# Expert loop of a two-layer kernel: rows turned by a transposing DMA, second product two tiles behind the first

## The reference

```
gate_scores = softmax(x @ Wg + bg);  topk_scores, topk_idx = top_k(gate_scores, 2)
for e in range(8):
    h = gelu(x @ W1[e] + b1[e])          # 128 -> 512
    y = h @ W2[e] + b2[e]                # 512 -> 128
    output = output + y * combine_w[..., e]
```

## Time and profile before

| | us |
|---|---|
| median of 3 runs | 1599.52 (1598.59 to 1602.85) |
| the profiled execution's own time | 1598.53 |
| its span, first to last instruction | 1596.6 |
| PE busy in the span | 1392.2 (87%) |
| DVE busy | 1355.3 (85%) |
| ACT busy | 1280.3 (80%) |
| POOL busy | 1079.0 (68%) |

### The profile page before, as it was taken

One profiled execution on the slowest core, in us unless ns is written; L12 is line 12 of the kernel. 1 busy time (PEld: TensorE's weight loads), 2 busy tenths in 40 slices (PEclk: granted clock), 3 DMA queues, 4 the chain that ended last, 5 costly groups with the idle time before them and its releaser, 6 DMA issues. The chain is left out here.

```text
span 1596.6 us, 53031 instructions
## 1 busy us (share of the span) xinstructions
PE 1392.2 (87%) x17084; PEld 1186.1 (74%) x17084; DVE 1355.3 (85%) x3979; ACT 1280.3 (80%) x3930; POOL 1079.0 (68%) x1524
## 2 busy tenths in 40 slices
PE   4779889974799999999999999999999719999970
PEld 3667777763688888888888888888888618888860
DVE  4479999995799999999999999999999628888877
ACT  1358888875799999999999999999999616666645
POOL 0367877763666577887788778877887555666650
PEclk7989999986899999999999999999999959999995
DMA  5445553400100000000000000000000013332209
GB/s 145 140 158 180 192 202 148 160 2 5 27 13 12 13 20 20 23 22 19 18 22 22 18 18 22 22 18 18 22 15 9 22 43 91 87 84 77 80 28 316
DMA packets 99738, 101.83 MB, mean 64 GB/s; under 512 B 15305, under 2 KB 81132, under 8 KB 99457
## 3 DMA queue, kind: packets, MB, share of 16 engines
q1 hardware_dynamic: 82496, 78.77, 15.4%
q0 software_dynamic: 8640, 16.93, 3.2%
q10 hardware_dynamic: 8448, 4.20, 0.9%
HBM read 39.40 MB, written 57.16 MB: 60 GB/s over the span
## 5 line engine op out<-in xcount | busy, mean ns | idle before, releaser
L1227 ACT ACTIVATE c_p<-bank,c_nmax 128x128 f32<-128x128 f32 x1024 | 368.9, 401 | 2.2 <-DVE c_nmax L1081 1.3
L1016 POOL TENSOR_TENSOR c_p<-c_p,c_rden 128x512 f32<-128x512 f32 x256 | 266.8, 1042 | 110.4 <-DVE c_rden L1091 106.0
L1227 ACT ACTIVATION_READ_ACCUMULATOR c_p<-bank,c_nmax 128x1 f32 x1024 | 244.2, 241 | 0.0
L1403 POOL DMA_INDIRECT moe_outputs<-e_y,e_to x142 | 152.9, 1077 | 93.3 <-DVE e_y L1434 58.6
L112 PE MATMUL bank<-c_kvT,qk_fused 128*128 128x128 f16 x1024 | 185.8, 220 | 10.8 <-ACT c_kvT L1206 10.4
L1081 DVE TENSOR_REDUCE c_nmax<-bank 128x4 f32<-128x512 f32 x256 | 173.4, 677 | 17.5 <-PE bank L114 14.3
L114 PE MATMUL bank<-c_kvT,qk_fused 128*128 128x128 f16 x1024 | 185.7, 220 | 0.0
L113 PE MATMUL bank<-c_kvT,qk_fused 128*128 128x128 f16 x1024 | 185.7, 220 | 0.0
L1473 ACT ACTIVATE e_h<-bank,moe_b 128x256 f32<-128x256 f32 x284 | 117.9, 466 | 65.7 <-PE bank L114 64.4
L1297 PE MATMUL bank<-const,c_p 128*128 128x128 f32 x1024 | 155.9, 275 | 3.6 <-DVE c_pT0rest L1102 1.7
L1059 POOL DMA_INDIRECT moe_slots<-r_rows,r_pos x128 | 131.6, 1028 | 34.9 <-issue 34.9
(11 more groups left out here) (324 smaller groups left out, 5921.0 us busy)
## 6 DMA issues: line engine op xcount, KB each, us to landing
moe_slots<-slot_fill SPq DMA_DIRECT2D x66, 520.0 KB, 5.6
e_rows<-moe_slots SPq DMA_DIRECT2D x71, 130.0 KB, 2.2
f_z<-moe_outputs SPq DMA_DIRECT2D x32, 256.0 KB, 4.9
x<-in_x SPq DMA_DIRECT2D x16, 256.0 KB, 3.2
a_ctx<-in_ctx SPq DMA_DIRECT2D x32, 128.0 KB, 3.4
moe_stage<-in_L_ffn_W SPq DMA_DIRECT2D x16, 256.0 KB, 3.1
c_rows<-in_ctx SPq DMA_DIRECT2D x128, 32.0 KB, 2.0
c_rows<-x SPq DMA_DIRECT2D x128, 32.0 KB, 1.8
```

The lines of the kernel that those rows point to most:

```text
L1016: pool.tensor_tensor(pr[r % 4][:], pr[r % 4][:], rep(rden[r % 4][:], 2, P), ALU.mult).then_inc(m["pn"], 1)
L1227: last = act.activation(pr[r % 4][:, h, :], SB[r % 2][:, P * h:P * h + P], ACT.Exp, bias=nmax[r % 4][:, h:h + 1], accum_out=den[r % 4][:, ...
L1403: pool.indirect_dma_start(s.z, bass.IndirectOffsetOnAxis(ap=to[t % YBUF][:, h:h + 1], axis=0), ys[t % YBUF][:, h, :], None, bounds_check=2 ...
```

## The change

SP issues two DMAs per tile where it issued one: a transposing one of the first 256 values of each slot, straight into `e_xT` (now 6 buffers, free again when the first product of tile t-6 is through), and a plain one of the last 4 half floats into `e_dest` (12 buffers). PE's `turn` and DVE's `spread` go away with their semaphores, and the two banks that they used go to the first product, which now turns over 6 banks instead of 4. `second` and `finish` run two tiles behind instead of one; the parts of h get a third set. The weights are addressed through a view with an axis for the expert, instead of `e * FF + P * b`.

```diff
-XBUF, YBUF = 12, 6
+XBUF, DBUF, YBUF = 6, 12, 6
...
-    hs = [[sb(f"e_hs{n}{part}", [P, KB, TSLOT], F16) for part in ("high", "rest")] for n in range(2)]
+    hs = [[sb(f"e_hs{n}{part}", [P, KB, TSLOT], F16) for part in ("high", "rest")] for n in range(3)]
...
-    HB, YB = s.pb[0:4], s.pb[4:6]
-    XTB = [s.pb[6][:].bitcast(F16), s.pb[7][:].bitcast(F16)]
+    HB, YB = s.pb[0:6], s.pb[6:8]
+    by_expert = wts[:].rearrange("p a (e f) -> p a e f", e=EXPERTS)
+
+    def bank(t, b):
+        return HB[(KB * t + b) % 6]
+
+    def weight(part, e, b):
+        return by_expert[:, part, bass.ds(e, 1), P * b:P * b + P].rearrange("p o c -> p (o c)")
...
                 if t >= XBUF:
-                    old = t - XBUF
-                    sp.wait_ge(m["xt2"], old + 1)
-                    sp.wait_ge(m["y_done"], old + 1)
+                    sp.wait_ge(m["h"], KB * (t - XBUF + 1))
+                if t >= DBUF:
+                    sp.wait_ge(m["y_done"], t - DBUF + 1)
                 row = sp.value_load(tab[0:1, 1, t:t + 1], min_val=0, max_val=XROWS - TSLOT)
-                sp.dma_start(xr[q][:], s.xs[bass.ds(row, TSLOT), :].rearrange("(h p) w -> p h w", p=P)).then_inc(x_in[q], 16)
+                sp.dma_start_transpose(xt[q][:], s.xs[bass.ds(row, TSLOT), 0:2 * D]).then_inc(x_in[q], 16)
+                sp.dma_start(xd[d][:], s.xs[bass.ds(row, TSLOT), 2 * D:ROW].rearrange("(h p) w -> p h w", p=P)).then_inc(d_in[d], 16)
...
-            def spread(t):
-                dve.wait_ge(m["x_t"], t + 1)
-                if t >= 2:
-                    dve.wait_ge(m["h"], 4 * (t - 1))
-                dve.tensor_copy(xt[t % 2][:].rearrange("p a c -> p (a c)"), XTB[t % 2][:, 0:2 * TSLOT]).then_inc(m["xt2"], 1)
...
-            spread(0)
-            for t in range(NTILE + 1):
+            for t in range(NTILE + 2):
                 if t == NTILE:
                     gates()
-                if t + 1 < NTILE:
-                    spread(t + 1)
                 if t < NTILE:
                     split(t)
-                if t > 0:
-                    finish(t - 1)
+                if t >= 2:
+                    finish(t - 2)
...
-            def turn(t):
+            def first(t, e):
                 pe.wait_ge(x_in[t % XBUF], 16 * (t // XBUF + 1))
-                if t >= 2:
-                    pe.wait_ge(m["xt2"], t - 1)
-                for part in range(2):
-                    for h in range(2):
-                        at = TSLOT * part + P * h
-                        last = pe.transpose(XTB[t % 2][:, at:at + P], xr[t % XBUF][:, h, D * part:D * part + D], s.ident_h[:])
-                last.then_inc(m["x_t"], 1)
-
-            def first(t, e):
-                pe.wait_ge(m["xt2"], t + 1)
-                x = [xt[t % 2][:, part, :] for part in range(2)]
+                x = [xt[t % XBUF][:, part, :] for part in range(2)]
                 for b in range(KB):
-                    if t:
-                        pe.wait_ge(m["gelu"], 4 * (t - 1) + b + 1)
-                    w = [wts[:, part, bass.ds(e * FF + P * b, P)] for part in range(2)]
-                    parts_product(pe, HB[b][:, 0:TSLOT], w, x).then_inc(m["h"], 1)
+                    if KB * t + b >= 6:
+                        pe.wait_ge(m["gelu"], KB * t + b - 5)
+                    parts_product(pe, bank(t, b)[:, 0:TSLOT], [weight(part, e, b) for part in range(2)], x).then_inc(m["h"], 1)
...
-            for t in range(NTILE + 1):
+            of = [None, None]
+            for t in range(NTILE + 2):
+                now = pe.value_load(tab[0:1, 0, t:t + 1], min_val=0, max_val=EXPERTS - 1) if t < NTILE else None
                 if t < NTILE:
-                    e = pe.value_load(tab[0:1, 0, t:t + 1], min_val=0, max_val=EXPERTS - 1)
-                    first(t, e)
-                if t + 1 < NTILE:
-                    turn(t + 1)
-                if t > 0:
-                    second(t - 1, old)
-                old = e
+                    first(t, now)
+                if t >= 2:
+                    second(t - 2, of[0])
+                of = [of[1], now]
```

More of the change, by code:

```diff
@@ L1353, in attend_and_route @@
     sem = s.sem
-    names = "x_t xt2 h gelu h_high h_split y y_done exp scaled combined stored"
+    names = "h gelu h_high h_split y y_done exp scaled combined stored"
     m = {n: sem("d_" + n) for n in names.split()}
     x_in = [sem(f"d_x_in{n}") for n in range(XBUF)]
+    d_in = [sem(f"d_dest_in{n}") for n in range(DBUF)]
     y_out = [sem(f"d_y_out{n}") for n in range(YBUF)]
@@ L1367, in attend_and_route @@
             sb2 = lambda name, shape, dt=F32: ctx2.enter_context(nc.sbuf_tensor(name, shape, dt))
-            apply_experts(nc, s, m, x_in, y_out, sb2, s.wts, tab, expert, picks, gate)
+            apply_experts(nc, s, m, x_in, d_in, y_out, sb2, s.wts, tab, expert, picks, gate)
         with ExitStack() as ctx2:
@@ L1371, in attend_and_route, with apply_experts @@
             combine(nc, s, m, z_in, sb2, gate, out)
-def apply_experts(nc, s, m, x_in, y_out, sb, wts, tab, expert, picks, gate):
-    xr = [sb(f"e_rows{n}", [P, 2, ROW], F16) for n in range(XBUF)]
-    xt = [sb(f"e_xT{n}", [P, 2, TSLOT], F16) for n in range(2)]
+def apply_experts(nc, s, m, x_in, d_in, y_out, sb, wts, tab, expert, picks, gate):
+    xt = [sb(f"e_xT{n}", [P, 2, TSLOT], F16) for n in range(XBUF)]
+    xd = [sb(f"e_dest{n}", [P, 2, 4], F16) for n in range(DBUF)]
     hf = [sb(f"e_h{n}", [P, KB, TSLOT]) for n in range(2)]
-    hs = [[sb(f"e_hs{n}{part}", [P, KB, TSLOT], F16) for part in ("high", "rest")] for n in range(2)]
+    hs = [[sb(f"e_hs{n}{part}", [P, KB, TSLOT], F16) for part in ("high", "rest")] for n in range(3)]
     ys = [sb(f"e_y{n}", [P, 2, D]) for n in range(YBUF)]
@@ L1506, in second @@
                     for b in range(KB):
-                        w = [wts[:, 2 + part, bass.ds(e * FF + P * b, P)] for part in range(2)]
-                        last = parts_product(pe, YB[t % 2][:, P * h:P * h + P], [part[:, b, P * h:P * h + P] for part in hs[t % 2]], w, b == 0, b == KB - 1)
+                        last = parts_product(pe, YB[t % 2][:, P * h:P * h + P], [part[:, b, P * h:P * h + P] for part in hs[t % 3]],
+                                             [weight(2 + part, e, b) for part in range(2)], b == 0, b == KB - 1)
                 last.then_inc(m["y"], 1)
-            turn(0)
-            old = None
-            for t in range(NTILE + 1):
+            of = [None, None]
+            for t in range(NTILE + 2):
+                now = pe.value_load(tab[0:1, 0, t:t + 1], min_val=0, max_val=EXPERTS - 1) if t < NTILE else None
                 if t < NTILE:
-                    e = pe.value_load(tab[0:1, 0, t:t + 1], min_val=0, max_val=EXPERTS - 1)
-                    first(t, e)
-                if t + 1 < NTILE:
-                    turn(t + 1)
-                if t > 0:
-                    second(t - 1, old)
-                old = e
+                    first(t, now)
+                if t >= 2:
+                    second(t - 2, of[0])
+                of = [of[1], now]
 def combine(nc, s, m, z_in, sb, gate, out):
```

23 lines of the change are left out of this document (12 added, 11 removed).

## The result

| | before | after |
|---|---|---|
| median of five runs each, us | 1602.64 (1598.59 to 1603.06) | 1588.55 (1582.44 to 1590.58) |
| ratio of the times | | 0.9921, 95% interval 0.9904 to 0.9938 |
| profiled execution, us | 1598.53 | 1582.44 |
| its span, us | 1596.6 | 1580.6 |

The kernel became 0.8% faster. The forecast was 1589, and the interval of the ratio lies wholly beyond the 0.3% that the prediction takes as no change. The mechanism is the one forecast, though the gain per tile is 0.20 us where 0.14 was forecast, and SP came far closer to setting the pace than was forecast.

The account below looks back on a forecast made before the run. PE's sequencer was taken as the bound. Steady tiles -9.4 us (3.23 to 3.09 per tile), start -3.4 and end +2.6 gave -10.2: 1588.3 for the profiled execution, 1589 for the runs, range 1566 to 1604.

Parts of the forecast that it names:

- What bounds the kernel: Expert loop: PE's sequencer, 3.11 of 3.23 us per tile, sets the pace; the array needs only 2.87.
- The lone wait: PE's wait ahead of the transposes, standing alone, goes with them: 0.13 us of sequencer per tile, counted in full.
- the irregular rest: The remaining 0.12 us per tile of PE's sequencer, dispatch and fetching, shrinks by 0.01 with 4 of some 40 products gone.
- The addresses: Weights addressed by expert block on PE: still 16 register instructions per tile, worth 0.
- DVE's copy: DVE's copy of 0.42 us per tile goes; DVE has idle time and nobody on PE waits for it: 0.
- The second product two behind: Second product two tiles behind, three sets, six banks: removes PE waits that have no row of weight when steady: 0.
- POOL's floor: POOL's two scatters and two gaps per tile take 2.75 us, staying under PE as the floor.
- SP and the DMA: Transposing DMA stays hidden behind 3.1 us per tile; one more issue costs SP 0.4 us, issued five tiles ahead: 0.
- SP is full: Sign that the DMA step is wrong: SP full, or PE waiting for e_xT from DMA in most tiles.
- rival C: The transposing DMA sets the pace once turn and load exceed 3.23 us per tile: 1610 to 1740 us; chance 0.19.
- The start: Loop start: PE runs first(0) to first(2) without a turn or second between, first(3) 4.5 us earlier, landing 1.1 later: -3.4 us.
- The end: Loop end: four scatters instead of two stand behind the gates on POOL's way to combine: +2.6 us.

Follow-up runs that it names:

- e9: Kernel before with PE's load of the expert without its range check, two register instructions fewer: 1586.3 us, ratio 0.9906.
- e3c: Kernel after with four more unused 128x128 transposes per tile on TensorE, one ahead of each block of the first product: 1589.8 us.
- e4c: Kernel after with two more waits ahead of the second product, for values reached long before, making one semaphore instruction more per tile: 1601.2 us.
- e2: Kernel after with second product, split and finish one tile behind the first again, and two sets of parts: 1594.4 us.
- e5: Kernel after with PE's load of the expert without its range check: 1575.6 us.
- e11: Kernel after with PE's wait for the landed rows moved to share the semaphore instruction ahead of the second product: 1579.6 us.
- e1: Kernel after with the weights addressed the old way, register times 512 plus a constant: 1589.3 us.
- e10: Kernel before with second product, split and finish two tiles behind and three sets of parts: 1601.6 us, ratio 1.000.
- e12: Kernel after with PE's and SP's loads unchecked, the shared wait for landed rows, and gates behind DVE's last finish: 1562.3 us.
- e4: Kernel after with one more wait ahead of the second product, for a value reached long before; no instruction was added: 1590.2 us.
- e6: Kernel after with PE's load of the expert and SP's load of the row both without range check: 1569.3 us.

## Why the prediction came out

*What bounds the kernel.* Right: the sequencer, not the array. Two register instructions taken out of it (e9) gain 13.5 us, four transposes put into the array (e3c) cost next to nothing. The working was off inside: the lone waits take 0.34 us and the load of the expert 0.65 at their shortest, not 0.39 and 0.72, so the rest in the kernel before is 0.23 us and not 0.12.

*The lone wait, -0.13 us; the irregular rest, -0.01.* The first is right (base -0.14, and e4c puts it back at +0.12). The second is the term that was mis-sized: 0.06. It was scaled with the number of products, and e3c shows that they have no part in it. It comes with one semaphore instruction more (e4c). The long steps are not scattered: in the kernel after, 72 of the 125 distances between two of them are exactly nine steps of the sequencer, and the commonest places in a tile are hit in one tile of three; in the kernel before, 69 of 181 are nine, and the commonest places are hit in one tile of two. That looks like something counted in instructions and not like an engine that is late, but no run tests it. Why the kernels with 22 steps have 0.21 to 0.23 us of it, and those with fewer 0.16 to 0.18 wherever no engine is late (e2, e5 and e9 have one), stays open: e11 has a step fewer than the change and lost nothing of it. So the period became 3.03 and not 3.09, and from the first product of tile 3 to that of tile 70 13.5 us were gained instead of 9.4.

*The addresses, 0.* Right: e1, and 16 register instructions per tile still.

*DVE's copy, 0.* Right as far as the runs go: e4c has no copy and takes the time of the kernel before, and in the kernel after PE's step in front of the second product is 0.105 to 0.106 us in every tile from 1330 to 1520. No run takes away the copy alone.

*The second product two behind: 0, none of it has a row.* Right in the sum of the change, wrong in its reason. It was read off the kernel before that PE doesn't wait for the split, and that is so (e10). But the cover was the turn, which the change takes away: e2 shows +0.10 us per tile, some 7 us, without the distance. The prediction asked what covers the new waits of DVE and ACT, and not what had covered the split; it also looked for PE's waits in a view that doesn't show what its sequencer waits for.

*POOL's floor, 2.75.* Somewhat high: 2.65 (e12), since two scatters at 0.98 and 1.06 with two gaps of 0.30 is what it needs when it is never held up. It lies under PE in the kernel after, as said.

*SP and the DMA: hidden.* Right in the outcome, wrong in the reason. The bounds were made from the DMA engines, with 0.378 us for the issue. The price is in the issue, 1.22 us. SP's round became 2.85 us against PE's 3.03, so that "with SP waiting most of the time" turned false, and the prediction's own sign of a wrong step, "SP is full", is nearly there: rival C was missed by 6%, and e5 runs into it. The lead was not four to five tiles either: it is one tile at the start and grows to five at the end. The engines themselves have room: the queue's 27.9% are 0.84 us of all engines per tile, against 0.56, and its packets are 822 per tile against 272, three times as many and not eight. The Trainium skill, "VectorE: DVE Perf Modes", section "The three transpose paths", has 1309 ns per 128x128 block by DMA, which in series would be an estimated 5.2 us for the four blocks of a tile; the runs have 2.85 us for a whole round of SP and 1.3 for a further turn of four blocks, so they do not agree with four blocks in series, and the measurement decides. The Trainium skill's other figure, 261 GB/s in "DMA: Bandwidth & Descriptors", section "Latency and other measured facts", is about the transfer, and no run here isolated that. SP's issue alone takes more than twice the 0.5 us that this figure would give as an estimate.

*The start, -3.4.* It was -2.0, counted from SP's first issue to the first product of tile 3 (12.02 against 14.05 us). Tile 0 came well, 2.84 us after its issue, where the kernel before took 3.3. But SP sends the next turn 2.7 us later, and PE stood 2.2 us ahead of tile 1. Here too the issue had been taken as 0.378 us. By its own test (first(3) before 1323) the step passes at 1320.60, but 2.3 us of that lie ahead of the loop; without them it would be 1322.9, at the very edge. The size of this term is uncertain: from SP's first issue to the load of tile 3 it is 13.2 us before and 11.2 after, but 12.0 to 12.3 in e1, e4 and e3c.

*The end, +2.6.* Right: four scatters 1.29 apart behind the gates; from the first product of tile 70 to the combine's first load it is 19.56 us instead of 17.24, +2.3.

*The sum.* Steady -13.5, start -2.0, end +2.3: -13.2, against the forecast -10.2. That the median came to within 1 us of the forecast is part luck: the gain in the loop was larger by 3, and the kernel before had a median of 1602.6 in the runs beside the kernel after, where the forecast took 1599.5. For the profiled execution the forecast was 1588.3 and it took 1582.44; half of that miss is the loop, the other half lies outside it.

## What to carry to other kernels

Where PE's products are small and their addresses come from registers, work out what its sequencer costs from start to start of its records. A semaphore instruction was worth 0.10 to 0.17 us here, so let waits share one (two fit, and the next instruction carries a third) before moving any work off the array. Before you take work away that stands between a producer and its consumer, ask what it covered. And price a new kind of DMA by what its issue holds the queue's engine, not only by the DMA engines' share.

## What the runs showed of the hardware

- The issue of a transposing DMA of 256 rows by 256 fp16 columns holds SP for 1.22 us (in the kernel after 1.21 at the least, 2.37 at the most), three times the plain issue's 0.378; a second one adds 1.3 us to SP's round.
- A semaphore instruction on PE carries two waits at the same 51 ns of record as one (e4). A wait doesn't lengthen the record of the instruction that carries it but puts off its start: in e2 and e9 the instruction that waits for DVE's split starts 38 to 40 ns after the split's end.
- One semaphore instruction costs between 0.10 (e11) and 0.17 us (e4c) per tile, and the second figure holds 0.06 us that appear as steps of 25 ns and more over the shortest, 2.8 per tile instead of 1.9; their origin is open.
- The range check of a value load costs PE's sequencer 0.27 (e5) to 0.29 us (e9) of its base, and SP 0.28 of its shortest round (e6: 2.27 against 2.55).
